# Conditions over another queue, other sums of magnitudes, two-term mixing and unread products in the first tile of an octonion ternary FFN

## Chip, cores and metric

One core of a Trainium2 chip runs the whole kernel. The metric is device time in microseconds of an execution. Three executions of the kernel before took 722.28 to 724.03 us, median 723.83.

## The reference, cut to what matters

```python
xc   = einsum('bct,bcd->bdt', x, weights[condition])      # x: 32 x 64 x 1024, one 64 x 64 matrix per batch entry
Wq   = scale * clip(round(W / scale), -1, 1)              # scale = mean(|W|), for w_gate, w_up, w_down
M    = einsum('jik,jod->koid', S_OCT, Wq)                 # octonion structure constants, 8 x 8 x 8
gate, up = xp @ M_gate, xp @ M_up                         # 1024 -> 2732 each
h    = silu(gate) * up
out  = x + hp @ M_down                                    # 2732 -> 1024
```

Every weight is first replaced by -1, 0 or 1 times the mean magnitude of its whole matrix, so no table of weights can be built before all magnitudes of that matrix are summed.

## The kernel before

The 2048 token rows are 8 tiles of 256. A tile goes through three stages: y (x times the condition's matrix), 12 chunks of gate and up, and the down products. The order of every engine is written out by hand; semaphores join them.

Weights: at the start w_gate (three windows, from ACT's queue) and w_up (three windows) and w_down (one transfer, both from SP's queue) come in as f32. `sum_abs` sums magnitudes (ACT, L672; one window of w_up on DVE, L906), PE adds the partitions (L968), DVE makes the scales (`scales`), then ternary f16 weights (`ternary`, L747 and L749) and from these tables of sums of two weights (`build_table`, L723 to L768). The tables of windows 1 and 2 are made between the first tile's chunks. w_down's ternary weights are combined on PE (`mix`, L981): each mix is four results, each a sum of four ternary blocks with signs, written as products with the identity or its negative; ACT copies them to `down_u` (L667), and scales 16 blocks to `down_c` (L705, `CORR_AFTER`).

y: `y_round(T, r)` (L1003) is 8 f32 products; ACT copies and squares them (`copy_y`, L588, L591), PE sums the squares (`row_norms`, L1010), DVE makes the tile's scales. POOL forms sums of y (`sum_y`, L531), ACT the high f16 parts (`y_hi`, L601), DVE the low parts (`y_lo`, L816). The four conditions of a tile are 64 x 64 blocks loaded into `cond_bd` by an index read from memory (`load_one_cond`, L457, L458); in tile 0 two come from SP's queue and two from ACT's.

Chunk c: PE makes shared products (`shared_pair`, `shared`) and own products (`own`, gate group then up group of 16, all L1016). DVE adds them (p, L723; gate and up, L843), ACT applies silu (L652), DVE multiplies (L870), and one chunk later ACT and DVE split the result into a high and low f16 part (L613, L825). POOL and DVE form sums z of these over groups of chunks; `z_hi` (ACT, L632) and `z_lo` (DVE, L830). The down products are L1108. In the first tile only, `first_tile_at(c, half)` puts y rounds of tile 1 and the 12 mixes before (half 0) or after (half 1) the own products of a chunk.

Of the kernel before, what the change touches and what calls it, by code (L numbers as in the profile page):

```python
# [159 lines left out]
def build(nc, x, cond, cond_w, w_gate, w_up, w_down, out, count):  # L160
# [16 lines left out]

    Y_AT_FIRST = {(1, 1): 0, (2, 1): 1, (3, 0): 2, (3, 1): 3}
    NORM_AT_FIRST = (4, 1)
# [8 lines left out]
    Z_LO_AFTER_FIRST = {8: 0, 9: 1, 10: 2, 11: 3}  # L188
    CORR_AFTER = (8, 9, 10, 11)
    MIX_AT = [(c, half) for c in range(6, 12) for half in range(2)]  # L190
# [24 lines left out]
    with ExitStack() as ctx:  # L215
# [44 lines left out]
        raw_down_at = z_op_f16[:, 2 * NQ * raw_n:].bitcast(F32)  # L260
        raw_down = [of_window(raw_down_at, w) for w in range(NQ)]
        tern_down_at = o_sb[:].rearrange("p a t -> p (a t)")[:, 0:NQ * raw_n // 2].bitcast(F16)
        tern_down = tern_down_at.rearrange("p (w j o) -> p w j o", w=NQ, j=8)
# [77 lines left out]
        idx_loaded = sem("idx_loaded")  # L341
        cond_loaded = sem("cond_loaded")
        x_loaded = sem("x_loaded")
        residual_loaded = [sem(f"residual_loaded_{s}") for s in range(SUB)]
# [11 lines left out]
        tern_ready = [sem("gate_tern_ready"), sem("up_tern_ready"), sem("down_tern_ready")]  # L356
        slots_built = [sem("gate_slots_built"), sem("up_slots_built")]
        down_mixed = sem("down_mixed")
        down_c_ready = sem("down_c_ready")
# [61 lines left out]
        for (h, v), f in F_SIGN.items():  # L421
            for r in range(4):
                r1, r0 = divmod(r, 2)
                terms = []
                for a in range(2):
                    first = 4 * (h ^ v) + 2 * a
                    sign = f[2 * a] * (1, parity(r1))[a]
                    other = parity(r0) if f[2 * a] == f[2 * a + 1] else -parity(r0)
                    terms += [(first, sign), (first + 1, sign * other)]
                mixes[h, v, r] = sorted(terms, key=lambda t: -t[1])  # L430
        MIXES = [(w, h, v) for w in range(NQ) for h, v in F_SIGN]
# [22 lines left out]

        def load_one_cond(eng, T, b):
            h = b % 2
            which = eng.value_load(idx_sb[0:1, T * BPT + b:T * BPT + b + 1], min_val=0, max_val=cond_w.shape[0] - 1)  # L457
            eng.dma_start(cond_bd[C * h:C * h + C, b // 2, C * h:C * h + C],  # L458
                          cond_w[bass.ds(which, 1), :, :].rearrange("a c d -> (a c) d")).then_inc(cond_loaded, 16)

# [3 lines left out]
        def _(sp):  # L464
# [6 lines left out]
            def load_cond(T):  # L471
                for b in range(BPT):
                    load_one_cond(sp, T, b)

# [13 lines left out]
            load_x(0)  # L488
            sp.wait_ge(idx_loaded, 16)
            sp.wait_ge(cond_zeroed, 1)  # L490
            for b in range(BPT // 2):
                load_one_cond(sp, 0, b)
            for w in range(NQ):
                sp.dma_start(raw[1][w], w_up[:, w]).then_inc(up_loaded[w], 16)
            sp.dma_start(raw_down_at, w_down.rearrange("p w j o -> p (w j o)")).then_inc(down_loaded, 16)
            load_x(1)
            load_cond(1)
            sp.wait_ge(down_mixed, len(MIXES))
# [20 lines left out]
        def _(pool):  # L519
# [6 lines left out]
            for dst, value in ((ident, 1.0), (minus_ident, -1.0)):  # L526
                pool.affine_select(out=dst[:], in_=dst[:], compare_op=ALU.not_equal, fill=value, base=0,
                                   pattern=[[-1, P]], channel_multiplier=1).then_inc(ident_set, 1)

            def signed_add(dst, a, b, sign):  # L530
# [52 lines left out]
        def _(act):  # L583
# [36 lines left out]
            def z_hi(T, k):  # L620
                if k == NR - 1:
                    act.wait_ge(z_ready_dve, T + 1)
                else:
                    act.wait_ge(z_ready, (NR - 1) * T + k + 1)
                if T == 0 and k % 2 == 0:


                    for m in range(2):
                        act.wait_ge(slots_built[m], NBUILD * min(NQ, k + 2))
                    if k > 0:  # L630
                        act.wait_ge(tern_ready[2], NQ)
                act.activation(z_op[:, k, 0], z_of(k), ACT.Copy).then_inc(z_hi_ready, 1)  # L632
# [40 lines left out]

            def sum_abs_of(m, w):
                act.wait_ge((gate_loaded, up_loaded)[m][w], 16)
                sum_abs(NQ * m + w, raw[m][w].rearrange("p j o -> p (j o)"), raw_n, abs_sum[m][:, w:w + 1])

            for w in range(NQ):
                act.dma_start(raw[0][w], w_gate[:, w]).then_inc(gate_loaded[w], 16)
            act.wait_ge(idx_loaded, 16)  # L680
            act.wait_ge(cond_zeroed, 1)
            for b in range(BPT // 2, BPT):
                load_one_cond(act, 0, b)
            act.wait_ge(ones_set, 1)
            act.activation(warm, ones[:, 0:1], ACT.Silu)
            for w in range(NQ):
                sum_abs_of(0, w)
            for r in range(4):
                copy_y(0, r)
            for w in range(NQ - 1):  # L690
                sum_abs_of(1, w)
            y_hi(0)
            act.wait_ge(down_loaded, 16)
            sum_abs(2 * NQ - 1, raw_down_at, NQ * raw_n, abs_sum[2])

            corr_list = list(corr.items())
            per_chunk = -(-len(corr_list) // len(CORR_AFTER))
            for T in range(NT):
                for c in range(NC):
                    chunk(T, c)  # L700
                    if T == 0 and c in CORR_AFTER:
                        act.wait_ge(tern_ready[2], NQ)
                        i = per_chunk * CORR_AFTER.index(c)
                        for (h, v, p), (_, ((j, eight),)) in corr_list[i:i + per_chunk]:
                            act.activation(down_c[:, :, v, p, h, :], tern_down[:, :, j, :], ACT.Copy,  # L705
                                           scale=float(eight)).then_inc(down_c_ready, 1)
# [14 lines left out]
        def _(dve):  # L721
# [176 lines left out]
            def ternary_of(m, w):  # L898
                ternary(m, w, tern[m][w], raw[m][w], next(n_tern))

            scales(0)
            ternary_of(0, 0)
            build_table(0, 0)
            y_scales(0)
            dve.wait_ge(up_loaded[NQ - 1], 16)
            dve.tensor_reduce(abs_sum[1][:, NQ - 1:NQ], raw[1][NQ - 1].rearrange("p j o -> p (j o)"), AX.X, ALU.add,  # L906
                              apply_absolute_value=True).then_inc(abs_summed_dve, 1)
            scales(1)
            scales_of_ffn()
            h_scales(0)  # L910
            y_lo(0, range(2))
            ternary_of(1, 0)
            build_table(1, 0)
            y_lo(0, range(2, NY))
            ternary_of(0, 1)
            for T in range(NT):
                for c in range(NC):
# [5 lines left out]
                    if T == 0:  # L923
                        if c in TERN_AFTER:
                            ternary_of(*TERN_AFTER[c])
                        if c in TABLE_AFTER:
                            build_table(*TABLE_AFTER[c])
                        if c in DOWN_AFTER:
                            w = DOWN_AFTER[c]
                            ternary(2, w, tern_down[:, w], raw_down[w], next(n_tern))  # L930
                    if T == 0 and c == SCALES_AFTER_FIRST:
                        scales_of_tile(1)
# [30 lines left out]
        def _(pe):  # L963
            def sum_abs(m):
                pe.wait_ge(abs_summed, (NQ, 2 * NQ - 1, 2 * NQ)[m])
                if m == 1:
                    pe.wait_ge(abs_summed_dve, 1)
                pe.matmul(totals(m), ones[:], abs_sum[m], start=True, stop=True).then_inc(totals_ready, 1)  # L968

            def mix(i):  # L970
                w, h, v = MIXES[i]
                pe.wait_ge(tern_ready[2], w + 1)
                if i == 0:
# [5 lines left out]
                for r in range(4):  # L979
                    for t, (j, sign) in enumerate(mixes[h, v, r]):  # L980
                        mm = pe.matmul(bank_mix[:, r, :], (ident if sign > 0 else minus_ident)[:], tern_down[:, w, j, :],  # L981
                                       start=(r == 0 and t == 0), stop=(t == 3), skip_group_check=True)
                mm.then_inc(down_mixed, 1)

            def y_round(T, r):
                if r == 0:
                    pe.wait_ge(x_loaded, 16 * (T + 1))
                    pe.wait_ge(cond_loaded, 16 * BPT * (T + 1))
                if T > 0:
# [152 lines left out]
            def down(T):  # L1142
# [19 lines left out]
                for s in range(SUB):  # L1162
                    down_part(s, down_u_of(2), False, True).then_inc(down_u_done, 1)

            pe.wait_ge(ones_set, 4)
            for r in range(2):
                y_round(0, r)
# [4 lines left out]

            sum_abs(1)
            for T in range(NT):
                for c in range(NC):
# [50 lines left out]
```

## Time and profile before

| | |
|---|---|
| runs, median (lowest to highest) | 723.83 us (722.28 to 724.03) |
| profiled execution | 724.41 us, span 722.6 us |
| PE busy | 687.3 us, 95% |
| DVE, ACT, POOL busy | 538.6, 332.3, 352.5 us |
| chain that ended last | PE 85%, DVE 7%, ACT 3% |
| granted PE clock, mean | 0.987 |

The span runs from the first to the last instruction of the program. A share of busy time is an average over stages. PE's granted clock is given as a part of 2.4 GHz: 0.50 is 1.2 GHz. The timeline of a stretch lists the instructions of each engine in order of time, neighbours of one kind merged, and in brackets how long the engine was idle before the first and what ended that.

### The profile page before, as it was taken

How to read it: one execution, taken by the hardware profiler on the slowest of the kernel's cores; microseconds unless marked ns; L12 is line 12 of the kernel's file. 1: busy time of each engine (PE TensorE's matmuls, PEld its weight loads, DVE VectorE, ACT ScalarE, POOL GpSimd, SP SyncE). 2: the span in 40 equal slices, each digit the busy share in tenths (PEclk: the TensorE clock that was granted, in tenths of full speed). 3: DMA queues.
4: the chain of work that ended last, by engine and by line, in shares of the span. 5: the costliest groups of instructions: out<-in, count | busy, mean ns of one | idle time of the engine just before them, and what ended most of it. 6: DMA issues, size and time to landing. Idle time of an engine off the chain costs nothing.

```text
span 722.6 us, 17130 instructions
## 1 busy us (share of the span) xinstructions
PE 687.3 (95%) x7046; PEld 625.0 (86%) x7046; DVE 538.6 (75%) x867; ACT 332.3 (46%) x530; POOL 352.5 (49%) x409
## 2 busy tenths in 40 slices
PE   3679998999999999999999999999999999999995
PEld 3468887999999989999899999999899998988895
DVE  1898956767876688676877678766877678777877
ACT  5543485155444546255452555344452554434531
POOL 0200557435736466344856356364753357464553
PEclk9799999999999999999999999999999999999999
DMA  8100003021002110031001110031000300021001
GB/s 327 59 2 1 1 2 122 30 89 64 1 2 88 33 61 2 2 118 63 1 2 52 66 63 2 2 117 62 4 1 11 108 2 1 2 88 31 1 2 59
DMA packets 10576, 31.51 MB, mean 44 GB/s; under 512 B 3330, under 2 KB 3330, under 8 KB 10370
## 3 DMA queue, kind: packets, MB, share of 16 engines
q1 hardware_dynamic: 9906, 28.81, 11.2%
q10 hardware_dynamic: 592, 1.61, 0.7%
q8 instruction: 56, 0.92, 0.5%
q14 instruction: 22, 0.18, 0.1%
HBM read 22.02 MB, written 8.39 MB: 42 GB/s over the span
## 4 chain that ended last, share of the span: by engine, by line
PE 85%; DVE 7%; ACT 3%; issue 2%; POOL 1%; DMA 1%; ACTq 0%; DVEq 0%; POOLq 0%
PE ps L1016 58%; PE ps L1108 21%; PE ps L1003 4%; DMA cond_bd<-in_L_cond_weights_dram 1%; DVE pu_sb L723 1%; ACT down_c L705 1%; POOL z_f L531 1%; PE ps L1010 1%; DVE o_sb L443 1%; ACT z_op L632 1%; DVE ps L843 1%; POOL h_pairs L531 1%; DVE z_op L830 0%; ACT ps L652 0%; DVE gate_table L723 0%
## 5 line engine op out<-in xcount | busy, mean ns | idle before, releaser
L1016 PE MATMUL ps<-y_op,gate_table 128*128 128x256 f16 x2112 | 273.0, 275 | 5.7 <-DVE y_op L816 4.2
L1016 PE MATMUL ps<-y_op,up_table 128*128 128x256 f16 x2112 | 270.7, 273 | 0.2 <-DVE up_table L768 0.2
L1016 PEld LDWEIGHTS ps<-y_op,gate_table 128*128 128x128 f16 x2112 | 207.6, 99 | 30.6 <-DVE y_op L816 4.3
L1016 PEld LDWEIGHTS ps<-y_op,up_table 128*128 128x128 f16 x2112 | 207.1, 98 | 25.1 <-DVE up_table L768 0.7
L531 POOL TENSOR_TENSOR h_pairs<-h_f 128x256 f32<-128x256 f32 (+1 forms) x128 | 121.1, 975 | 151.8 <-ACT h_f L618 94.1
L531 POOL TENSOR_TENSOR z_f<-h_pairs 128x512 f32<-128x512 f32 x80 | 102.7, 1305 | 102.6 <-DVE z_op L830 100.8
L652 ACT ACTIVATE ps<-ps,small 128x512 f32<-128x512 f32 x96 | 63.6, 662 | 175.5 <-DVE ps L843 125.4
L443 POOL TENSOR_TENSOR o_sb<-o_sb,wd_sb 128x256 f32<-128x256 f32 (+1 forms) x150 | 88.3, 626 | 92.7 <-DVE wd_sb L891 91.5
L1108 PE MATMUL ps<-down_c,h_op 128*128 128x128 f16 x1536 | 93.1, 220 | 3.0 <-ACT down_c L705 3.0
L723 DVE TENSOR_TENSOR pu_sb<-ps,q_sb 128x512 f32<-128x512 f32 x96 | 65.8, 686 | 38.7 <-ACT q_sb L646 26.0
L1108 PEld LDWEIGHTS ps<-down_c,h_op 128*128 128x128 f16 x1536 | 89.8, 98 | 4.0 <-ACT down_c L705 3.1
L1108 PE MATMUL ps<-down_u,z_op 128*128 128x256 f16 x768 | 90.8, 274 | 1.5 <-DVE z_op L830 1.5
L830 DVE TENSOR_TENSOR z_op<-z_f,z_op 128x1024 f16<-128x1024 f32 x40 | 49.8, 1246 | 44.7 <-ACT z_op L632 44.7
L825 DVE TENSOR_TENSOR h_op<-ps,h_op 128x512 f16<-128x512 f32 x96 | 65.8, 685 | 23.0 <-ACT h_f L618 23.0
L1108 PEld LDWEIGHTS ps<-down_u,z_op 128*128 128x128 f16 x768 | 73.9, 98 | 9.8 <-DVE z_op L830 1.6
L870 DVE SCALAR_TENSOR_TENSOR ps<-pu_sb,small,ps 128x512 f32<-128x512 f32 x96 | 72.4, 755 | 11.5 <-ACT ps L652 1.6
L613 ACT ACTIVATE h_op<-ps 128x512 f16<-128x512 f32 x96 | 57.5, 599 | 35.3 <-DVE ps L870 33.7
L843 DVE TENSOR_TENSOR pu_sb<-ps,pu_sb 128x512 f32<-128x512 f32 x72 | 49.4, 686 | 31.2 <-PE ps L1016 31.0
L632 ACT ACTIVATE z_op<-z_f 128x1024 f16<-128x1024 f32 x40 | 42.1, 1053 | 36.9 <-POOL z_f L531 36.9
L618 ACT ACTIVATE h_f<-ps 128x512 f32<-128x512 f32 x96 | 57.7, 601 | 0.0
L843 DVE TENSOR_TENSOR ps<-ps,pu_sb 128x512 f32<-128x512 f32 x72 | 49.8, 691 | 4.2 <-PE ps L1016 3.2
L1003 PE MATMUL ps<-cond_bd,x_in 128*128 128x128 f32 x256 | 35.3, 285 | 13.3 <-DMA cond_bd<-in_L_cond_weights_dram 11.1
(75 smaller groups left out, 480.7 us busy)
## 6 DMA issues: line engine op xcount, KB each, us to landing
x_in<-in_x_dram SPq DMA_DIRECT2D x8, 1024.0 KB, 5.3
o_sb<-in_x_dram SPq DMA_DIRECT2D x16, 512.0 KB, 3.6
out_dram<-o_sb SPq DMA_DIRECT2D x15, 512.0 KB, 2.7
h_op<-in_L_ffn_w_gate_dram ACTq DMA_DIRECT2D x3, 512.0 KB, 6.8
h_op<-in_L_ffn_w_up_dram SPq DMA_DIRECT2D x3, 512.0 KB, 7.4
z_op<-in_L_ffn_w_down_dram SPq DMA_DIRECT2D x1, 1536.0 KB, 11.4
out_dram<-o_sb SPq DMA_DIRECT2D x2, 256.0 KB, 2.1
cond_bd<-in_L_cond_weights_dram SPq DMA_DIRECT2D x30, 16.0 KB, 3.0
```

The lines of the kernel that those rows point to most:

```text
L443: last = eng.tensor_tensor(dst, dst, wd_sb[:, s, k1, r0, h, :], ALU.add if sign > 0 else ALU.subtract)
L531: return pool.tensor_tensor(dst, a, b, ALU.add if sign > 0 else ALU.subtract)
L613: act.activation(h_op[:, c, :, 0, :], bank_r(s, 0), ACT.Copy).then_inc(h_hi_ready, 1)
L618: act.activation(h_f[:, c], bank_r(s, 0), ACT.Copy).then_inc(h_copied, 1)
L652: act.activation(bank_r(s, 0), bank_r(s, 0), ACT.Silu, scale=gate_scale(T)).then_inc(silu_ready, 1)
L723: return dve.tensor_tensor(dst, a, b, ALU.add if sign > 0 else ALU.subtract)
L825: dve.tensor_tensor(h_op[:, c, :, 1, :], bank_r(s, 0), h_op[:, c, :, 0, :], ALU.subtract).then_inc(h_lo_ready, 1)
L843: return dve.tensor_tensor(dst, bank, pm.broadcast_to([P, 2, TOK]), ALU.add)
L870: dve.scalar_tensor_tensor(out=bank_r(s, 0), in0=u_sb[:], scalar=up_scale(T), in1=bank_r(s, 0), op0=ALU.mult, op1=ALU.mult).then_inc(h_rea ...
L1003: mm = pe.matmul(bank_y(T, r)[:, i, P * s:P * s + P], x_in[:, s, f:f + P], cond_bd[:, s, :], start=True, stop=True)
L1016: mm = pe.matmul(dst, table[m][:, slot, q, :], y_op[:, op, e, :], start=(i == 0 and e == 0), stop=(i == len(terms) - 1 and e == 1))
L1108: mm = pe.matmul(banks[bank][:, place], operand[:, P * s:P * s + P], weights, start=(bank not in begun), stop=(last and i == ends[bank]), ...
```

## The change

It does six things. (1) The four conditions of tile 0 are issued by POOL, after its set-up, with a semaphore of their own; SP and ACT issue none, and SP goes straight on to w_up and w_down. (2) DVE sums the magnitudes of w_up's windows 0 and 1 before all else, ACT that of window 2 after the copies of y. (3) DVE's order up to the first chunk is changed. (4) Rounds of y for tile 1 stand at other places, all before the own products. (5) DVE adds and subtracts neighbouring ternary blocks of w_down (`down_pairs`), and a mix is a sum of two terms in place of four; the waits of `z_hi` follow from where `down_pairs` lies. (6) Corrections are 6, 5 and 5 behind chunks 8, 9 and 10, in place of 4 behind each of 8 to 11; and PE makes 14 products of 512 columns before y and 4 behind the sum for w_up, into a bank whose content nobody reads.

```diff
-    Y_AT_FIRST = {(1, 1): 0, (2, 1): 1, (3, 0): 2, (3, 1): 3}
+    Y_AT_FIRST = {(1, 0): 0, (2, 0): 1, (3, 0): 2, (4, 0): 3}
-    CORR_AFTER = (8, 9, 10, 11)
+    CORR_AFTER = {8: range(0, 6), 9: range(6, 11), 10: range(11, 16)}
...
+        down_pairs = [raw_down_at[:, w * raw_n:w * raw_n + raw_n // 2].bitcast(F16).rearrange("p (j o) -> p j o", j=8)
+                      for w in range(NQ)]
...
-                    first = 4 * (h ^ v) + 2 * a
+                    pair = 2 * (h ^ v) + a
-                    terms += [(first, sign), (first + 1, sign * other)]
-                mixes[h, v, r] = sorted(terms, key=lambda t: -t[1])
+                    terms.append((pair if other > 0 else 4 + pair, sign))
+                mixes[h, v, r] = terms
...
             load_x(0)
-            sp.wait_ge(idx_loaded, 16)
-            sp.wait_ge(cond_zeroed, 1)
-            for b in range(BPT // 2):
-                load_one_cond(sp, 0, b)
             for w in range(NQ):
                 sp.dma_start(raw[1][w], w_up[:, w]).then_inc(up_loaded[w], 16)
...
+            pool.wait_ge(idx_loaded, 16)
+            pool.wait_ge(cond_zeroed, 1)
+            for b in range(BPT):
+                load_one_cond(pool, 0, b, first_cond_loaded)
...
-                if T == 0 and k % 2 == 0:
+                if T == 0 and k < NQ:
                     for m in range(2):
-                        act.wait_ge(slots_built[m], NBUILD * min(NQ, k + 2))
-                    if k > 0:
-                        act.wait_ge(tern_ready[2], NQ)
+                        act.wait_ge(slots_built[m], NBUILD * (k + 1))
+                elif T == 0:
+                    act.wait_ge(down_mixed, 4 * (k - NQ + 1))
...
-            act.wait_ge(idx_loaded, 16)
-            act.wait_ge(cond_zeroed, 1)
-            for b in range(BPT // 2, BPT):
-                load_one_cond(act, 0, b)
...
             for r in range(4):
                 copy_y(0, r)
-            for w in range(NQ - 1):
-                sum_abs_of(1, w)
+            sum_abs_of(NQ, 1, NQ - 1)
             y_hi(0)
...
+            for w in range(NQ - 1):
+                dve.wait_ge(up_loaded[w], 16)
+                dve.tensor_reduce(abs_sum[1][:, w:w + 1], raw[1][w].rearrange("p j o -> p (j o)"), AX.X, ALU.add,
+                                  apply_absolute_value=True).then_inc(abs_summed_dve, 1)
             scales(0)
             ternary_of(0, 0)
             build_table(0, 0)
             y_scales(0)
-            dve.wait_ge(up_loaded[NQ - 1], 16)
-            dve.tensor_reduce(abs_sum[1][:, NQ - 1:NQ], raw[1][NQ - 1].rearrange("p j o -> p (j o)"), AX.X, ALU.add,
-                              apply_absolute_value=True).then_inc(abs_summed_dve, 1)
             scales(1)
+            ternary_of(1, 0)
+            y_lo(0, range(2))
+            build_table(1, 0)
+            y_lo(0, range(2, NY))
             scales_of_ffn()
             h_scales(0)
-            y_lo(0, range(2))
-            ternary_of(1, 0)
-            build_table(1, 0)
-            y_lo(0, range(2, NY))
             ternary_of(0, 1)
...
                             ternary(2, w, tern_down[:, w], raw_down[w], next(n_tern))
+                            dve.wait_ge(tern_ready[2], w + 1)
+                            t = tern_down[:, w]
+                            for place, sign in ((slice(0, 4), 1), (slice(4, 8), -1)):
+                                signed_add(down_pairs[w][:, place], t[:, 0::2], t[:, 1::2], sign).then_inc(down_paired, 1)
...
-                        mm = pe.matmul(bank_mix[:, r, :], (ident if sign > 0 else minus_ident)[:], tern_down[:, w, j, :],
-                                       start=(r == 0 and t == 0), stop=(t == 3), skip_group_check=True)
+                        mm = pe.matmul(bank_mix[:, r, :], (ident if sign > 0 else minus_ident)[:], down_pairs[w][:, j, :],
+                                       start=(r == 0 and t == 0), stop=(t == 1), skip_group_check=True)
...
+            def unread(n):
+                for _ in range(n):
+                    pe.matmul(ps[:, 5, 0:4 * P], ones_bf[:], ones_bf[:].rearrange("p (a o) -> p a o", a=1)
+                              .broadcast_to([P, 4, P]), start=True, stop=True)
+
             pe.wait_ge(ones_set, 4)
+            unread(14)
             for r in range(2):
                 y_round(0, r)
             sum_abs(0)
...
             sum_abs(1)
+            unread(4)
```

## Rows read from the trace of the kernel before

**Rows 1.** The waits of PE, 136 to 722 us: releaser, us in total, times, longest.
```profile
PE ps L1108 <- DVE z_op L830: 1.5, 1, 1.5
```

**Rows 2.** The waits of PE, 0 to 140 us.
```profile
PE ps L1003 <- ACT y_sq L591: 2.2, 1, 2.2
```

**Rows 3.** The timeline, 75 to 120 us: start, us, instruction, idle before.
```profile
84.97 2.17 DVE L749 SCALAR_TENSOR_TENSOR o_sb<-z_op,small,o_sb 128x1024 f16<-128x1024 f32 x1
...
87.07 0.68 DVE L723 TENSOR_TENSOR pu_sb<-ps,q_sb 128x512 f32<-128x512 f32 x1
...
90.12 1.75 ACT L705 ACTIVATE down_c<-o_sb 128x384 f16<-128x384 f16 x4
...
92.84 1.22 DVE L830 TENSOR_TENSOR z_op<-z_f,z_op 128x1024 f16<-128x1024 f32 x1 [2.41 <-ACT z_op L632]
...
93.98 0.68 DVE L723 TENSOR_TENSOR pu_sb<-ps,q_sb 128x512 f32<-128x512 f32 x1
...
112.56 2.95 PE L1108 MATMUL ps<-down_c,h_op 128*128 128x128 f16 x32 [2.98 <-ACT down_c L705]
```

**Rows 4.** The timeline, 0 to 36 us, and chunk 3's gate products.
```profile
2.95 1.84 SPq L458 DMA_DIRECT2D cond_bd<-in_L_cond_weights_dram  x2
...
4.83 1.53 SPq L494 DMA_DIRECT2D h_op<-in_L_ffn_w_up_dram  x3
...
11.06 3.58 PE L1003 MATMUL ps<-cond_bd,x_in 128*128 128x128 f32 x16 [11.06 <-DMA cond_bd<-in_L_cond_weights_dram]
...
14.80 0.16 DVE L729 TENSOR_REDUCE small<-ps 128x1 f32<-128x3 f32 x1 [14.80 <-PE ps L968]
...
19.29 4.12 POOL L531 TENSOR_TENSOR y_f<-y_f 128x256 f32<-128x256 f32 x5 [16.88 <-DVE gate_table L768]
...
20.13 1.21 DVE L906 TENSOR_REDUCE small<-h_op 128x1 f32<-128x1024 f32 x1
...
23.72 2.47 DVE L816 SCALAR_TENSOR_TENSOR y_op<-y_f,small,y_op 128x1024 f16<-128x1024 f32 x2
...
26.25 3.60 PE L1016 MATMUL ps<-y_op,gate_table 128*128 128x256 f16 x16 [4.20 <-DVE y_op L816]
26.89 1.28 DVE L749 SCALAR_TENSOR_TENSOR z_op<-h_op,small,z_op 128x1024 f16<-128x1024 f32 x1
...
28.21 1.16 DVE L723 TENSOR_TENSOR up_table<-z_op 128x512 f16<-128x512 f16 x4
...
29.92 1.80 DVE L816 SCALAR_TENSOR_TENSOR y_op<-y_f,small,y_op 128x1536 f16<-128x1536 f32 x1
...
34.47 0.69 DVE L723 TENSOR_TENSOR pu_sb<-ps,q_sb 128x512 f32<-128x512 f32 x1 [0.76 <-PE ps L1016]
...
51.64 3.39 PE L1016 MATMUL ps<-y_op,gate_table 128*128 128x256 f16 x16
```

**Rows 5.** The waits of DVE, 0 to 66 us.
```profile
DVE small L729 <- PE ps L968: 15.5, 2, 14.8
DVE pu_sb L843 <- PE ps L1016: 2.0, 2, 1.2
DVE ps L843 <- PE ps L1016: 1.9, 1, 1.9
```

**Rows 6.** Issue to landing, us: x's (last number), then w_up's, then the conditions'.
```profile
x_in<-in_x_dram SPq DMA_DIRECT2D x1, 1024.0 KB, 8.1
...
DMA to landing us min/median/max: 6.7/7.4/8.2
...
DMA to landing us min/median/max: 2.0/5.0/7.0
```

**Rows 7.** Stretches: PE, PEld, DVE, ACT, POOL busy, granted clock, DMA share, GB/s.
```profile
50.00:60.00 10.00, 9.35 (x70) 7.93 (x71) 6.83 (x16) 5.42 (x12) 0.00 (x0) 0.83 0.01 2
...
113.00:136.00 23.00, 23.00 (x290) 21.53 (x288) 16.68 (x17) 8.04 (x10) 9.56 (x9) 0.93 0.28 96
```

**Rows 8.** The chain of waits, 80 to 90 us: start, us, what.
```profile
81.39 0.89 PE ps L981 x16
```

More of the change, by code:

```diff
@@ L342, in build @@
         cond_loaded = sem("cond_loaded")
+        first_cond_loaded = sem("first_cond_loaded")
         x_loaded = sem("x_loaded")
@@ L357, in build @@
         slots_built = [sem("gate_slots_built"), sem("up_slots_built")]
+        down_paired = sem("down_paired")
         down_mixed = sem("down_mixed")
@@ L458, in load_one_cond @@
             eng.dma_start(cond_bd[C * h:C * h + C, b // 2, C * h:C * h + C],
-                          cond_w[bass.ds(which, 1), :, :].rearrange("a c d -> (a c) d")).then_inc(cond_loaded, 16)
+                          cond_w[bass.ds(which, 1), :, :].rearrange("a c d -> (a c) d")).then_inc(loaded, 16)
         block = ctx.enter_context(nc.Block())
@@ L472, in load_cond @@
                 for b in range(BPT):
-                    load_one_cond(sp, T, b)
+                    load_one_cond(sp, T, b, cond_loaded)
             def rows(T, s):
@@ L496, in _ @@
             load_x(1)
+            sp.wait_ge(idx_loaded, 16)
+            sp.wait_ge(cond_zeroed, 1)
             load_cond(1)
@@ L672, in sum_abs, with sum_abs_of @@
                 act.activation(junk[:, 0:size], src, ACT.Abs, accum_out=dst).then_inc(abs_summed, 1)
-            def sum_abs_of(m, w):
+            def sum_abs_of(n, m, w):
                 act.wait_ge((gate_loaded, up_loaded)[m][w], 16)
-                sum_abs(NQ * m + w, raw[m][w].rearrange("p j o -> p (j o)"), raw_n, abs_sum[m][:, w:w + 1])
+                sum_abs(n, raw[m][w].rearrange("p j o -> p (j o)"), raw_n, abs_sum[m][:, w:w + 1])
             for w in range(NQ):
                 act.dma_start(raw[0][w], w_gate[:, w]).then_inc(gate_loaded[w], 16)
-            act.wait_ge(idx_loaded, 16)
-            act.wait_ge(cond_zeroed, 1)
-            for b in range(BPT // 2, BPT):
-                load_one_cond(act, 0, b)
             act.wait_ge(ones_set, 1)
@@ L686, in _ @@
             for w in range(NQ):
-                sum_abs_of(0, w)
+                sum_abs_of(w, 0, w)
             for r in range(4):
                 copy_y(0, r)
-            for w in range(NQ - 1):
-                sum_abs_of(1, w)
+            sum_abs_of(NQ, 1, NQ - 1)
             y_hi(0)
             act.wait_ge(down_loaded, 16)
-            sum_abs(2 * NQ - 1, raw_down_at, NQ * raw_n, abs_sum[2])
+            sum_abs(NQ + 1, raw_down_at, NQ * raw_n, abs_sum[2])
             corr_list = list(corr.items())
-            per_chunk = -(-len(corr_list) // len(CORR_AFTER))
             for T in range(NT):
@@ L702, in _ @@
                         act.wait_ge(tern_ready[2], NQ)
-                        i = per_chunk * CORR_AFTER.index(c)
-                        for (h, v, p), (_, ((j, eight),)) in corr_list[i:i + per_chunk]:
+                        for i in CORR_AFTER[c]:
+                            (h, v, p), (_, ((j, eight),)) = corr_list[i]
                             act.activation(down_c[:, :, v, p, h, :], tern_down[:, :, j, :], ACT.Copy,
@@ L964, in sum_abs @@
             def sum_abs(m):
[L965 removed]
+                pe.wait_ge(abs_summed, NQ + m)
                 if m == 1:
[L967 removed]
+                    pe.wait_ge(abs_summed_dve, NQ - 1)
                 pe.matmul(totals(m), ones[:], abs_sum[m], start=True, stop=True).then_inc(totals_ready, 1)
@@ L971, in mix @@
                 w, h, v = MIXES[i]
-                pe.wait_ge(tern_ready[2], w + 1)
+                pe.wait_ge(down_paired, 2 * (w + 1))
                 if i == 0:
@@ L987, in y_round @@
                     pe.wait_ge(x_loaded, 16 * (T + 1))
-                    pe.wait_ge(cond_loaded, 16 * BPT * (T + 1))
+                    if T == 0:
+                        pe.wait_ge(first_cond_loaded, 16 * BPT)
+                    else:
+                        pe.wait_ge(cond_loaded, 16 * BPT * T)
                 if T > 0:
```

2 lines of the change are left out of this document (1 added, 1 removed).

## The prediction

> **What bounds the kernel now.** I read the waits of TensorE (PE) first, in two stretches. After the first tile PE waits once, 1.5 us in total [rows 1]; every other wait of weight lies in the first 136 us, as 2.2 us for a square of y [rows 2]; the timelines give the rest in brackets: 3.0 us for down_c [rows 3], 11.1 for the first conditions, 4.2 for y's operands [rows 4]. From the first down product at 112.56 us [rows 3] on, PE has no gap, so the end moves by what that product moves, plus changes of PE's clock around it. The diff touches nothing behind it. The question is thus: how much earlier does down(0) start?
>
> Ahead of it, the timeline by engine shows who carries the chain. VectorE (DVE) starts at 14.80 us [rows 4] and then waits for PE's sum only once, 15.5 - 14.8 = 0.7 us, before the scales of up. Then PE and DVE alternate; in chunks 3 and 4 DVE waits for PE 1.9 us, and twice more, 2.0 together [rows 5]. In chunks 5 to 7 DVE never waits. In chunks 8 to 11 it waits for ScalarE (ACT) before every z_lo, 2.41 us in the first [rows 3]: silu, mix copy, four corrections, z_hi, then z_lo, then the next chunk. That loop takes 93.98 - 87.07 = 6.9 us.
>
> **Start of the chain.** x, ahead of all else on SP's queue, lands 8.1 us after its issue [rows 6], so past 9. The four conditions go out from 2.95 on, two on each queue, and take up to 7.0 us; PE starts at 11.06 [rows 4, 6]. The first 16 y products take 3.58 us, and PE granted at full level would take half: I read it as its lower level, 1.2 GHz. DVE's first scale stands behind them: 11.06 to 14.80 = 3.74 us. In the new kernel two sums of 1.21 us stand ahead of it on DVE. The second of the three up transfers is issued near 5.3 (three in the 1.53 us from 4.83) and takes 7.4 us, landing at 12.7 [rows 4, 6]; the queues are already full of earlier bytes, so the earlier issue in the new order shifts the landing little. 12.7 + 1.21 = 13.9; I take 14.0 against 14.80: 0.8 us gained. This holds if the conditions land by 14.0 - 3.74 = 10.3. No row shows a transfer issued by GpSimd (POOL). Bounds: four issues in a row at SP's pace (4.83 - 2.95 over two = 0.94 each) from 2.4, when POOL's last set-up ends, give 6.2; with the fastest landing of a condition, 2.0, they are there at 8.2, and x decides, past 9; with the slowest, 7.0, at 13.2, 2.9 too late. I take the median landing of 5.0: 11.2, and then count on the 14 unread products: they start at about 1.7 us, 0.43 us each at 1.2 GHz, and if they bring PE to 2.4 GHz the first 16 take 1.8 instead of 3.6, so that 12.1 is early enough. So 0 cost, bounds 0 and +2.9.
>
> The Trainium skill ("DMA: Bandwidth & Descriptors", SWDGE vs HWDGE vs iDMA) says that a POOL transfer has its descriptors written in software and that plain transfers belong on SP or ACT; its latency section gives about 1 us against 0.6 to the first byte. By that figure the conditions would be some 0.4 us later, inside the slack above. No run here shows it yet.
>
> **To y and chunk 0.** Out of DVE's chain go the sum of up's third window (1.21 us [rows 4], now on ACT at about 17, behind the copies of y) and the hole of 0.7, since the totals are now there early. The ffn and h scales (about ten small instructions, the scales of up among them, stand between the hole's end at 22.1 and 23.72; 1.1 us is theirs) move behind the last y_lo. The ternary of up (2.1 us) moves ahead of the first two y_lo. y_lo 0 starts at 23.72 - 0.8 - 1.2 - 0.7 - 1.1 + 2.1 = 22.0. POOL's sums of y (4.12 us) follow the gate table and now lie beside that ternary. The same ternary step took 1.28 us alone and 2.17 us beside POOL in chunk 7 [rows 3, 4]; bounds 0 and 0.9, I take 0.5. Two y_lo: 2.47. Ready at 25.0; PE's first gate group started at 26.25. The table of up (28.21 to 29.92: 1.8 with its wait) is ready at 26.8, the last y_lo (1.8) at 28.6 (before 31.7) [rows 4]. Scales and ternary(0,1) leave DVE free at 31.8.
>
> PE decides chunk 0. sum_abs(1) and its four unread products are over by 20, then PE idles until 25. In the trace it idled 4.2 us there and the first 16 products took 3.60 us, the lower level. I take the same fall. Then gate ends at 28.6, PE rises near 30, up ends at 31.1, the 16 shared ones at 32.85. DVE's chunk 0 starts at 32.85 against 34.47: **-1.6 us** (bounds: -2.7 if PE stays at 2.4 GHz and DVE decides, 0 if the rise comes 1.7 later).
>
> The Trainium skill ("SBUF — State Buffer", Who interferes with whom) says that a DVE instruction with two SBUF inputs and a POOL one that reads SBUF exclude each other. The 1.28 and 2.17 us agree. By it the ternary could wait for a whole POOL instruction, about 0.8 us, instead of my 0.5.
>
> **Chunks 0 to 5.** The first pairing adds two 128x512 f16 additions; four such take 1.16 [rows 4], two with their wait 0.6, on DVE with nothing beside: **+0.6 us** (bounds 0.5 and 0.8). y's first round of tile 1 now stands ahead of own(1) and waits for the scales of down, 3.2 us after chunk 0 begins: PE idles some 2.2 us there. Queued behind it is own(1), whose gate result DVE wants only 9 us after chunk 0 begins (chunk, scales, table, ternary, pairing), so it is late for nobody even at 1.2 GHz. In return rounds 1, 2 and 3 stand ahead of own(2), own(3), own(4), each a chunk half after ACT's squares: PE no longer holds for the square (2.2 us idle [rows 2], after which 16 products took 3.39 us [rows 4], with a mean granted clock of 0.83 from 50 to 60 [rows 7], that is 3.4 us at 0.50). By my walk own(3)'s gate is ready 2 us before DVE asks. So the waits 1.9 + 2.0 [rows 5] go, with rounding **-3.85 us**; the bound on the other side is 0, if the clock falls elsewhere or the hole only moves. I take the upper end, since 2 us of slack stand at each of three chunks. What is late next is DVE itself.
>
> **Chunks 6 and 7.** Two more pairings on DVE's chain, 0.6 each, now beside POOL, which has begun on z; 0.3 more each for the exclusion: **+1.8 us** (bounds +1.1 and +2.6).
>
> **Chunks 8 to 11.** Half of the mixing products go: 16 took 0.89 us [rows 8], so 12 x 0.44 = 5.3 us of PE. All of it is hidden: ACT's loop is the longer. Bounds 0 and -0.8. Corrections 4,4,4,4 become 6,5,5,0. One is 1.75/4 = 0.44 us [rows 3]: chunks 8, 9, 10 lengthen by 0.88 + 0.44 + 0.44 = 1.75, and the last four, which down(0) awaited, go with their 1.75. Net **0**. Next late is the copy of the last mix, 1.7 us earlier in its chunk. z_hi's new waits are on mixes long done; POOL's sums for tile 1 had some 5 us of slack before PE's second tile and keep over 3.
>
> **Sum.** -1.6 + 0.6 - 3.85 + 1.8 + 0 = -3.05 us. Against the profiled execution's 724.41 (span 722.6 and 1.8 around it) that is 721.4; the median of the runs is 0.6 lower, so **720.8**.
>
> **Rivals.**
> (B) The hole of chunks 3 and 4 does not go but moves: an idle PE at y's first round (2.2 us, as long as the one that half speed followed) brings the fall there. Then -1.6 + 0.6 + 1.8 = +0.8: 724.6, or anything between. For it: same length of idling. Against: slack of 2 us.
> (C) PE keeps 2.4 GHz where it lost it: at 25 (another -1.1, DVE decides) and behind 112.56, where the mean clock of 0.93 over 23 us [rows 7] is 3.2 us at 0.50, a loss of 1.6. -3.05 - 1.1 - 1.6 = -5.75: 718.1. For it: the unread products and shorter waits. Against: PE idles 5 us before y, and 2.3 us before down.
> (A) **Slower: POOL's issues decide.** Place: the four conditions. Each us after 10.3 (12.1 with PE at full speed) goes straight through y, first scale and DVE's chain. The gain of 3.05 is gone when they land at 13.4 (15.2); at 16 the time is 723.83 + 16 - 10.3 - 3.05 = 726.5. It needs about 3 us per issue from 2.4 on. For it: the four stand in a row on one queue and no row prices one. Against: nothing else is on POOL's queue then, and DVE is idle until 12.
>
> **Chances.** Forecast 0.45 (own range 719.6 to 722.3), B 0.20, C 0.25, A 0.10. About 0.3% (2.2 us) is what a measurement of this kernel can tell from no change; faster means below 721.7. Forecast gives 0.37 faster and 0.08 same, C 0.25 faster, B 0.20 same, A half same and half slower: 0.62, 0.33, 0.05. Range 717.8 (C) to 724.1 (most of B).
>
> **What would show it.** Conditions landed by 10.3 to 12.1; DVE's first scale at 14.0 and no hole before the second; first gate product at 25.0; chunk 0 on DVE at 32.9; no DVE wait for PE in chunks 3 and 4; the chunk loops 8 to 10 of 7.8, 7.3 and 7.3 us; down(0) at 109.5, released by the last mix copy. Wrong it would be made by a first y product behind 13, a clock at 0.50 between 35 and 60, or pairings of over a us.

## The result: slower by half a per cent

The changed kernel took 726.79 us (median, 725.95 to 727.35) against 722.88 us for the kernel before (722.08 to 724.03), each executed six times. The ratio is 1.0051, 95% interval 1.0039 to 1.0063: 3.7 us slower, where 3.05 us faster was forecast. Its profiled execution took 726.86 us, span 725.1. The waits of PE from 0 to 140 us in the profile after (columns as in [rows 2]):

```profile
PE ps L988 <- ACT down_u L675: 8.9, 6, 2.7
PE ps L1026 <- DVE y_op L818: 6.6, 1, 6.6
PE ps L1013 <- DMA cond_bd<-in_L_cond_weights_dram: 5.0, 1, 5.0
PE ps L1013 <- DVE small L735: 2.4, 1, 2.4
PE ps L1118 <- ACT down_u L675: 2.2, 1, 2.2
```

The wait for a square of y [rows 2] is gone and so is down_c's. In their place PE waits 8.9 us for copies of mixes: in chunks 6 to 11 PE is the engine that waits, not the one that sets the pace. After 136 us it waits 1.5 us once, as before [rows 1], so the loss lies in the first tile here too. The timeline of the changed kernel's start, answering to [rows 4]:

```profile
1.82 5.40 PE L1179 MATMUL ps<-ones_bf 128*128 128x512 bf16 x14 [1.82 <-POOL minus_ident L527]
...
3.69 0.66 POOL L463 DMA_DIRECT2D cond_bd<-in_L_cond_weights_dram  x1 [1.16 <-issue]
...
4.87 0.52 POOL L463 DMA_DIRECT2D cond_bd<-in_L_cond_weights_dram  x1 [0.51 <-issue]
...
6.01 0.52 POOL L463 DMA_DIRECT2D cond_bd<-in_L_cond_weights_dram  x1 [0.62 <-issue]
...
7.15 0.52 POOL L463 DMA_DIRECT2D cond_bd<-in_L_cond_weights_dram  x1 [0.63 <-issue]
...
12.23 3.75 PE L1013 MATMUL ps<-cond_bd,x_in 128*128 128x128 f32 x16 [5.01 <-DMA cond_bd<-in_L_cond_weights_dram]
12.61 1.22 DVE L905 TENSOR_REDUCE small<-h_op 128x1 f32<-128x1024 f32 x1 [0.16 <-DMA h_op<-in_L_ffn_w_up_dram]
...
16.24 0.16 DVE L731 TENSOR_REDUCE small<-ps 128x1 f32<-128x3 f32 x1 [2.42 <-PE ps L975]
...
20.73 5.42 POOL L539 TENSOR_TENSOR y_f<-y_f 128x256 f32<-128x256 f32 x5 [13.07 <-DVE gate_table L770]
20.86 1.02 PE L1179 MATMUL ps<-ones_bf 128*128 128x512 bf16 x4
...
22.20 1.71 DVE L749 TENSOR_SCALAR z_op<-h_op,small 128x1024 f16<-128x1024 f32 x1
23.95 1.62 DVE L751 SCALAR_TENSOR_TENSOR z_op<-h_op,small,z_op 128x1024 f16<-128x1024 f32 x1
25.50 2.93 DVE L818 SCALAR_TENSOR_TENSOR y_op<-y_f,small,y_op 128x1024 f16<-128x1024 f32 x2
...
28.49 3.60 PE L1026 MATMUL ps<-y_op,gate_table 128*128 128x256 f16 x16 [6.60 <-DVE y_op L818]
...
36.51 0.69 DVE L725 TENSOR_TENSOR pu_sb<-ps,q_sb 128x512 f32<-128x512 f32 x1 [1.54 <-PE ps L1026]
```

Read it in order. POOL's four issues start 1.14 us apart and the first only at 3.69; the last one's condition lets y begin at 12.23, not at 11.06. The 14 unread products end at 7.2, PE then idles 5.01 us, and the 16 y products take 3.75 us, the lower level (1.2 GHz) as before. So the first scale is at 16.24, with a hole of 2.42 us ahead of it on DVE, where 14.0 was forecast. Then three DVE steps fall under POOL's sums of y (20.73 on): 1.71, 1.62 and 2.93 us, where the kernel before had 0.75, 1.28 and 2.47.

DVE in chunks 6 to 9 of the changed kernel, answering to [rows 3]:

```profile
79.12 0.74 DVE L749 TENSOR_SCALAR o_sb<-z_op,small 128x1024 f16<-128x1024 f32 x1
79.89 1.63 DVE L751 SCALAR_TENSOR_TENSOR o_sb<-z_op,small,o_sb 128x1024 f16<-128x1024 f32 x1
81.55 1.70 DVE L725 TENSOR_TENSOR z_op<-o_sb 128x512 f16<-128x512 f16 x2
83.17 0.68 DVE L725 TENSOR_TENSOR pu_sb<-ps,q_sb 128x512 f32<-128x512 f32 x1
...
86.77 1.59 DVE L749 TENSOR_SCALAR o_sb<-z_op,small 128x1024 f16<-128x1024 f32 x1
88.39 2.17 DVE L751 SCALAR_TENSOR_TENSOR o_sb<-z_op,small,o_sb 128x1024 f16<-128x1024 f32 x1
90.60 0.76 DVE L725 TENSOR_TENSOR z_op<-o_sb 128x512 f16<-128x512 f16 x2
91.27 0.68 DVE L725 TENSOR_TENSOR pu_sb<-ps,q_sb 128x512 f32<-128x512 f32 x1
...
97.81 1.23 DVE L832 TENSOR_TENSOR z_op<-z_f,z_op 128x1024 f16<-128x1024 f32 x1 [3.17 <-ACT z_op L640]
```

A pairing is two additions, 0.76 us where POOL does not run beside it, 1.70 where it does; and the ternary step beside it (0.75 before, in chunk 7) now takes 1.59. The start of each of DVE's chunks, read from rows like these, and that of the first down product (down(0), on PE) give the ledger (us; "base" is the kernel of the experiments `y_places_and_corrections` and `base_again`, the latter's profile):

| chunk | 0 | 1 | 2 | 3 | 4 | 5 | 6 | 7 | 8 | 9 | 10 | 11 | down(0) |
|---|---|---|---|---|---|---|---|---|---|---|---|---|---|
| before | 34.47 | 41.66 | 47.01 | 52.00 | 60.45 | 68.25 | 73.60 | 80.91 | 87.07 | 93.98 | 100.91 | 107.77 | 112.56 |
| changed | 36.51 | 44.49 | 49.84 | 55.43 | 60.97 | 68.77 | 74.12 | 83.17 | 91.27 | 98.95 | 106.29 | 113.56 | 116.76 |
| changed - before | 2.0 | 2.8 | 2.8 | 3.4 | 0.5 | 0.5 | 0.5 | 2.3 | 4.2 | 5.0 | 5.4 | 5.8 | 4.2 |
| base | 34.19 | 41.38 | 46.74 | 51.72 | 56.99 | 64.80 | 70.15 | 77.47 | 83.62 | 91.37 | 98.71 | 105.98 | 109.18 |

Chunk 0 starts 2.0 us late, the three pairings add 0.8, 1.7 and 1.9, the y rounds give back 2.9 in chunk 3, and the corrections cost 1.6 and return it. That makes 3.5; the other 0.6 arise in chunk 2, where the kernel before has no wait:

```profile
39.81 1.45 PE L1013 MATMUL ps<-cond_bd,x_in 128*128 128x128 f32 x8 [2.40 <-DVE small L735]
41.05 3.29 PE L1026 MATMUL ps<-y_op,gate_table 128*128 128x256 f16 x16
...
52.26 0.69 DVE L845 TENSOR_TENSOR pu_sb<-ps,pu_sb 128x512 f32<-128x512 f32 x1 [0.53 <-PE ps L1026]
```

PE idles 2.40 us ahead of y's first round, then falls to its lower level (mean granted clock 0.57 from 40 to 44 us; the 16 gate products of chunk 1 take 3.29 us, and 1.91 at the higher level), and DVE still waits for it in chunk 2. This is rival B of the prediction, in part.

In this pair of profiles 1.7 of the 4.2 us come back behind 116.76: the first 32 down products took 1.95 us where they took 2.95 [rows 3], and the next 32 start 3.53 us behind them and not 5.19, PE being at its higher level.

### The profile page after: what moved, and what is told of

Same layout as the page of the kernel before. It is cut to its first block, busy times and chain, and to the rows that moved or that the text cites. A ratio compares the mean times of both kernels' runs of the same rounds, so it can differ in the third digit from the quotient of the medians.

```text
span 725.1 us, 16979 instructions
## 1 busy us (share of the span) xinstructions
PE 688.7 (95%) x6968; PEld 621.4 (86%) x6968; DVE 546.4 (75%) x874; ACT 331.7 (46%) x528; POOL 355.2 (49%) x413
## 4 chain that ended last, share of the span: by engine, by line
PE 85%; DVE 6%; ACT 3%; issue 2%; POOL 1%; DMA 1%; POOLq 0%; DVEq 0%; ACTq 0%
PE ps L1026 59%; PE ps L1118 21%; PE ps L1013 4%; ACT down_c L707 1%; PE ps L1020 1%; DVE pu_sb L725 1%; POOL z_f L539 1%; DVE o_sb L448 1%; ACT z_op L640 1%; DMA cond_bd<-in_L_cond_weights_dram 1%; DVE ps L845 1%; DVE ps L872 1%; DVE o_sb L751 1%; POOL h_pairs L539 1%; DVE z_op L832 0%
## 5 line engine op out<-in xcount | busy, mean ns | idle before, releaser
L539 POOL TENSOR_TENSOR y_f<-y_f 128x256 f32<-128x256 f32 (+1 forms) x40 | 41.0, 1048 | 13.7 <-DVE gate_table L770 13.1
```

The costliest lines, as they stand in the source:

```text
L539: return pool.tensor_tensor(dst, a, b, ALU.add if sign > 0 else ALU.subtract)
```

## The experiments

"Share of before" is the ratio of times to the kernel before on the same chip, with its 95% interval; 0.1% is 0.72 us. The first four undo one part of the changed kernel (its own share: 1.0051).

**Conditions back on SP's and ACT's queues.**

```diff
-            for b in range(BPT): load_one_cond(pool, 0, b, first_cond_loaded)
+            for b in range(BPT // 2): load_one_cond(sp, 0, b, first_cond_loaded)      # behind load_x(0)
+            for b in range(BPT // 2, BPT): load_one_cond(act, 0, b, first_cond_loaded) # behind w_gate
```

> The changed kernel with part 1 undone: two conditions from SP's queue and two from ACT's, as before. Theory (the start waits for POOL's conditions): y's first product comes back from 12.2 to about 11.1 us and DVE's first scale from 16.2 to 14.8 to 15.1, so the kernel is 1.0 to 1.4 us faster than the changed one: 725.4 to 725.8. Rival (the conditions hide behind up's two sums on DVE, which end at 13.8, and something later decides): under 0.3 us, 726.5 to 726.8.

Measured 1.0019 (1.0005 to 1.0032), 725.21 us: 2.3 us better than the changed kernel. y starts at 10.82, the first scale at 14.83, chunk 0 at 34.21, 2.3 us earlier. The rival (the conditions hide behind up's two sums) is out. The price is more than the 1.4 us at the first scale; part of it is made between the scale and chunk 0, where chunk 0 waited for PE 1.5 us in the changed kernel and 0.6 here, the gate products being 3.60 and 3.52.

**Mixes of four terms, no pairing.**

```diff
-                            for place, sign in ((slice(0, 4), 1), (slice(4, 8), -1)):
-                                signed_add(down_pairs[w][:, place], t[:, 0::2], t[:, 1::2], sign).then_inc(down_paired, 1)
...
-                        mm = pe.matmul(..., down_pairs[w][:, j, :], ...)   # 2 terms
+                        mm = pe.matmul(..., tern_down[:, w, j, :], ...)    # 4 terms
```

> The changed kernel with part 5 undone: no pairing on DVE, mixes of four terms on PE. Theory (DVE carries the chain in chunks 0, 6 and 7, and each pairing costs 0.8 to 1.7 us there, with what it pushes under POOL): DVE's chunk 8 starts 3.5 to 4.2 us earlier, down(0) too, and the time is 722.6 to 723.3. Rival (PE needs the 5.3 us of shorter mixes in chunks 6 to 11, so the pairing pays for itself): 726 or more.

Measured 0.9985 (0.9976 to 0.9994), 722.66 us: 4.8 us better, by itself enough to make the rest slightly faster than before. Chunk 8 starts at 86.79 in place of 91.27. The halved mixes bought nothing that the whole ones lack. Not all of the 4.8 us is the pairings', though. In this profile chunk 0 starts at 35.71, 0.8 us earlier before any pairing is made, and chunk 4 follows it after 24.45 us, with the first pairing after 24.46: PE fell behind y's first round in both, and what the missing pairing leaves free DVE spends in waiting for PE. The other 3.7 us lie in chunks 6 and 7.

**Sums and DVE's order as before.**

```diff
-            for w in range(NQ - 1): dve.wait_ge(up_loaded[w], 16); dve.tensor_reduce(abs_sum[1][:, w:w + 1], ...)
...
-            scales(1); ternary_of(1, 0); y_lo(0, range(2)); build_table(1, 0); y_lo(0, range(2, NY)); scales_of_ffn(); h_scales(0)
+            dve.tensor_reduce(abs_sum[1][:, NQ - 1:NQ], ...)
+            scales(1); scales_of_ffn(); h_scales(0); y_lo(0, range(2)); ternary_of(1, 0); build_table(1, 0); y_lo(0, range(2, NY))
```

> The changed kernel with parts 2 and 3 undone: magnitudes and DVE's order up to the first chunk as before, conditions still from POOL. Theory (the new order gains the sum and the hole, but its ternary and its first y_lo fall under POOL's sums of y: 1.71, 1.62 and 2.93 us for 0.74, 1.28 and 2.47): the two nearly cancel, first gate product within 0.7 us of the changed kernel's 28.5, time 726.0 to 727.3. Rival A (the order is worth the 2.5 us that its instructions say): 1.5 to 2.5 us slower than the changed kernel, over 728. Rival B (the order is itself the loss): 725.5 or less.

Measured 1.0034 (1.0022 to 1.0046), 726.06 us: 1.2 us better, with intervals that touch. The first gate product is at 27.39 in place of 28.49; 0.3 of these 1.1 us lie ahead of the first scale already (15.93 and 16.24). The order is not worth the 2.5 us that its instructions say (rival A is out), and is nearer to a loss.

**Without the unread products.**

```diff
-            unread(14)
...
-            unread(4)
```

> The changed kernel without the 18 unread products. Theory (they bring nothing: the first 16 y products took 3.75 us with them and 3.58 without, the first gate group 3.60 and 3.60): time within 0.5 us of the changed kernel, 726.3 to 727.3. Rival A (they keep PE at 2.4 GHz somewhere, as from 20.6 to 27 us): 1 us or more slower. Rival B (they hold PE's queue at y's start): 0.5 to 1 us faster.

Measured 1.0049 (1.0035 to 1.0063): no difference. The first 16 y products took 3.75 us and the first gate group 3.60, both ways.

The next ones build up from the kernel before.

**The places of y's rounds alone.**

```diff
-    Y_AT_FIRST = {(1, 1): 0, (2, 1): 1, (3, 0): 2, (3, 1): 3}
+    Y_AT_FIRST = {(1, 0): 0, (2, 0): 1, (3, 0): 2, (4, 0): 3}
```

> The kernel before with only part 4: rounds of y for tile 1 ahead of own(1), own(2), own(3), own(4). Theory (this part alone takes away the hole of 2.2 us on PE, the fall of the clock behind it and 3 us of DVE's waits in chunk 3; in all four kernels that have it chunk 3 to 4 takes 5.55 us against 8.45): 2.5 to 4 us faster than before, 720 to 721.5. Rival (the hole only moves to y's first round, where PE waits 2.4 us for the scales of down and falls to 1.2 GHz): within 1 us of before.

Measured 0.9973 (0.9962 to 0.9984), 721.33 us: 2.0 us faster (the median of 721.33 suggests more). In its profile chunk 3 takes 5.28 us in place of 8.45 and down(0) starts at 109.39 in place of 112.56, and the clock stays at 1.00 from 40 to 60 us. The rival's wait stands at y's first round, 2.40 us, but in this profile the 16 gate products behind it take 1.91 us and DVE sees nothing of it. That is not so in every execution, as the two profiles of the next kernel show; of the eleven of this one, seven took 720.8 to 721.5 us at a mean clock of 0.989 to 0.991, four 722.5 to 724.3 at 0.983 to 0.987.

**Places of y and corrections.**

```diff
-    CORR_AFTER = {8: range(0, 4), 9: range(4, 8), 10: range(8, 12), 11: range(12, 16)}
+    CORR_AFTER = {8: range(0, 6), 9: range(6, 11), 10: range(11, 16)}
```

> The kernel before with parts 4 and the corrections of part 6 (6, 5, 5, 0). Theory (what the three longer chunk loops of ACT cost, 1.2 to 1.7 us, the missing four at the end give back): within 0.5 us of the kernel with part 4 alone. Rival (PE's shorter wait before the down products keeps it at 2.4 GHz there, where the kernel before lost 1.6 us): 1 to 1.6 us faster than part 4 alone.

> The kernel with y's places and the corrections only, timed again as the base of the other three. Its runs so far fell into two groups, 719.5 (mean granted clock 0.994) and 721 to 721.8 (0.989). Expected: ratio to before 0.993 to 0.996, about 3 to 4.5 us faster than before. Rival (the gain over y's places alone was luck of three good runs): ratio 0.9965 or more.

Measured 0.9943 (0.9930 to 0.9955) and, a second time, 0.9953 (0.9940 to 0.9965): 3.4 to 4.1 us faster than before, and the fastest kernel found. The start of down(0) is no earlier than with y's places alone; what differs is PE behind it. First its first 32 down products with y's places alone, then with the corrections moved:

```profile
109.39 3.21 PE L1115 MATMUL ps<-down_c,h_op 128*128 128x128 f16 x32 [2.97 <-ACT down_c L709]
```

```profile
109.18 1.95 PE L1115 MATMUL ps<-down_c,h_op 128*128 128x128 f16 x32 [1.72 <-ACT down_u L672]
```

PE waits 1.72 us in place of 2.97 and comes out at its higher level; the next 32 start 3.53 us behind the first and not 4.79. The two stretches 105 to 125 us (columns: length, PE busy, granted clock, DMA share, GB/s), in the same order:

```profile
105.00:125.00 20.00, 17.03 (x217) 0.91 0.31 110
```

```profile
105.00:125.00 20.00, 18.28 (x253) 1.00 0.30 110
```

The fall costs 4.79 - 3.53 = 1.26 us in these rows; the ratios give 1.4 to 2.2. The rival is right: what the corrections bring is the clock behind the wait, not an earlier down(0). All six profiles with a wait of 1.7 us ahead of down(0) have 1.95 us for the first 32 products, the two with 3.0 us have 2.95 and 3.21. In between the length of the wait does not decide alone: behind 2.16 us five profiles have 1.95 and one 2.50.

The two profiles of this one kernel also show what rival B of the prediction is worth. The second (719.32 us) is "base" in the ledger; the first took 721.84 us. Its down(0) comes at 111.67, 2.5 us later, the whole difference. Of that 0.85 stand at chunk 0 (35.04 and 34.19; the first gate group took 3.60 and 3.30 us), and 1.7 in chunks 1 to 3, where its PE fell behind y's first round:

```profile
38.34 1.24 PE L1010 MATMUL ps<-cond_bd,x_in 128*128 128x128 f32 x8 [2.40 <-DVE small L737]
39.38 3.51 PE L1023 MATMUL ps<-y_op,gate_table 128*128 128x256 f16 x16
```

In the second profile the idling is the same 2.40 us, and the 16 products take 1.91 us.

**Sums and DVE's order with early conditions.** The base with parts 2 and 3 added.

```diff
-            dve.tensor_reduce(abs_sum[1][:, NQ - 1:NQ], ...)                 # behind y_scales(0)
+            for w in range(NQ - 1): dve.tensor_reduce(abs_sum[1][:, w:w + 1], ...)   # ahead of scales(0)
```

> Parts 2, 3, 4 and the corrections, with conditions as before, mixes of four terms and no unread products. It tells what the sums and DVE's order are worth once the conditions are early. Theory (the order gains little, since its ternary and first y_lo fall under POOL's sums of y): DVE's chunk 0 within 0.5 us of 34.4 and the time within 0.7 us of the kernel with parts 4 and corrections alone. Rival A (the order was only held up by the late conditions): 1.5 us or more faster than that one. Rival B (it is a loss of 1 us or more by itself).

Measured 0.9962 (0.9949 to 0.9974), 721.20 us. Chunk 0 starts at 34.25 (base 34.19 and 35.04). The first two y_lo take 2.94 us here too. It is 0.6 to 1.4 us behind the base's two measurements, inside the intervals of one and not of the other: no gain, and whether it is a loss stays open.

**POOL held back** while DVE makes the pairings.

```diff
-                    pool.wait_ge(slots_built[1], NQ * NBUILD)
+                    pool.wait_ge(down_paired, 2 * NQ)
```

> The changed kernel with POOL's first z round held until the last pairing is done (it began beside ternary and pairing of w_down's window 1). Theory (DVE's two-input instructions lose to POOL's on what they share): without POOL beside them the ternary steps take 0.74 and 1.28 us again instead of 1.59 and 2.17, each pairing 0.6 to 0.8 us for two instead of 1.70, and DVE's chunk 8 starts 2.3 to 3 us earlier, near 88.5; z is then late and ACT waits for it in chunk 8, so the time is the same or worse. Rival (the instructions are slow for where their operands lie): durations unchanged.

DVE in chunks 6 to 9 of this kernel:

```profile
79.41 0.74 DVE L749 TENSOR_SCALAR o_sb<-z_op,small 128x1024 f16<-128x1024 f32 x1
80.18 1.28 DVE L751 SCALAR_TENSOR_TENSOR o_sb<-z_op,small,o_sb 128x1024 f16<-128x1024 f32 x1
81.50 0.76 DVE L725 TENSOR_TENSOR z_op<-o_sb 128x512 f16<-128x512 f16 x2
...
85.78 0.75 DVE L749 TENSOR_SCALAR o_sb<-z_op,small 128x1024 f16<-128x1024 f32 x1
86.56 1.28 DVE L751 SCALAR_TENSOR_TENSOR o_sb<-z_op,small,o_sb 128x1024 f16<-128x1024 f32 x1
87.88 0.76 DVE L725 TENSOR_TENSOR z_op<-o_sb 128x512 f16<-128x512 f16 x2
88.56 0.68 DVE L725 TENSOR_TENSOR pu_sb<-ps,q_sb 128x512 f32<-128x512 f32 x1
...
95.20 1.37 DVE L832 TENSOR_TENSOR z_op<-z_f,z_op 128x1024 f16<-128x1024 f32 x1 [3.27 <-ACT z_op L640]
```

Every instruction has its duration back: 1.59 becomes 0.75, 2.17 becomes 1.28, the pairings are 0.76 each. Chunk 7 takes 6.4 us in place of 8.1, and chunk 8 starts at 88.56 in place of 91.27. The rival (where the operands lie) is out: operands and instructions are the same, only POOL is away. What is left of the two pairings, 0.5 us in chunk 6 and 0.2 in chunk 7 against the kernel before, is their own work, less what POOL had cost there before. As expected z is late and ACT's loop 8 takes 7.9 us in place of 7.7; one execution took 726.42 us, too near the changed kernel's to tell it apart.

**The three disputed parts, each on the base alone.** The diffs are those above the other way round.

> The base with the pairing and the mixes of two terms. Theory (the price of the pairing is DVE's and POOL's and has nothing to do with late conditions): 3.7 to 4.8 us slower than the base, as undoing it in the changed kernel gained 4.8. Rival (it only hurts because everything else is late too): under 2 us.

Measured 1.0001 (0.9992 to 1.0010), 724.55 us: 3.5 us slower than `base_again` (0.48%), a little under the expected 3.7 to 4.8. Chunk 8 starts at 89.49 in place of 83.62, and chunks 6 and 7 alone are longer by 3.5 us. So the price of the pairings in chunks 6 and 7 does not depend on late conditions; the rest of the shift to 89.49 arises up to chunk 3, where this profile, too, has PE at its lower level behind y's first round (3.26 us for the 16 gate products).

> The base with the four conditions issued by POOL. Theory (POOL's issues 1.14 us apart from 3.7 on bring y's first product to 12.2 to 12.5, and nothing hides that, since here no sum on DVE stands ahead of the first scale): 1.0 to 1.6 us slower than the base. Rival (in the changed kernel 2.3 us came back when it was undone, as the clock too was hurt): over 2 us.

Measured 0.9959 (0.9947 to 0.9971), 720.83 us: the interval overlaps the base's 0.9953. In the profiles, both with a mean clock of 0.994, y begins at 12.52 in place of 10.96 and down(0) at 111.06 in place of 109.18, and the executions at that clock took 720.6 to 721.1 us against 719.3 to 719.8. So 1.2 us on equal clocks, as the theory has it, but not shown by the medians, where the base had three executions of six at a mean clock of 0.989, 1.0 to 2.3 us longer, and this kernel one. In the base's two profiles, one from each group, PE falls behind y's first round in the longer and not in the shorter. That every execution of a group is like its profile is not shown.

> The base with the 18 unread products. Theory (they leave PE's level at y and at the first gate group as it was, since PE idles again behind them): within 0.5 us of the base. Rival (with the sums and order of the kernel before, the four behind sum_abs(1) stand only 3 us ahead of the first gate group, near enough to keep it at 2.4 GHz): first gate group 1.9 us in place of 3.6, and 1 us or more faster than the base.

Measured 0.9946 (0.9933 to 0.9958), 719.71 us: the same as the base within the intervals. The four stand close to the first gate group now, and still:

```profile
22.54 1.02 PE L1176 MATMUL ps<-ones_bf 128*128 128x512 bf16 x4
26.89 3.56 PE L1023 MATMUL ps<-y_op,gate_table 128*128 128x256 f16 x16 [3.33 <-DVE y_op L820]
```

PE waits 3.33 us behind them and works at its lower level again.

## Why the prediction was wrong

It named the right stretch and the right carriers and got the sign wrong. The start of down(0) was forecast 3.05 us earlier and came 4.2 later. Of these 7.3 us, 2.2 are the conditions and 1.4 the rest of the way to chunk 0, 2.1 the pairings, 1.0 y's places, and 0.6 the fall behind y's first round; 1.7 us came back behind down(0) in the profiles. By its own steps:

- **Pairings, +0.6 and +1.8: mis-sized by 2.1 us.** They cost 0.8 in chunk 0 and 1.7 + 1.9 in chunks 6 and 7, 4.5 us in the ledger, the largest cost of the change; undone, 4.8 us by the ratios, not all of it theirs, and 3.5 on the base. The step that failed is "0.3 more each for the exclusion". Beside POOL's additions a DVE instruction takes up to 1.0 us longer: the first pairing beside it took 1.70 for 0.76, and the one-input ternary step, which was given no price, 1.59 for 0.75. Holding POOL back gave both their durations back, so the cause is shown. The section of the Trainium skill that I weighed ("SBUF — State Buffer", Who interferes with whom) names that case as well: beside two-input instructions it lists tensor_scalar among those that can enter a mode with both ports and then contend with POOL. The trace agrees, with 1.59 and 0.75; that this instruction ran in that mode is not shown. I had read from the section only the two-input half.
- **Start of the chain, -0.8 and "0 cost" for the conditions: failed.** The first scale came at 16.24, 1.44 late. Two assumptions broke. The issues started at 3.69, not 2.4, as POOL reads each index and then issues, 1.14 us apart; the landing, 5.2 us behind the issue in the median of the four, was near the 5.0 that I took. And the 14 unread products did not bring y to the higher level, and PE idled 5.0 us between them and y. Undone, this part gives 2.3 us in the changed kernel and 1.2 to 1.9 on the base. The rival "POOL's issues decide" had the mechanism at a smaller size, and its break-even of 13.4 was not reached: alone it would not have turned the sign.
- **To y and chunk 0, -1.6: failed, measured +2.0.** Of the difference of 3.6, 2.2 are the start above (16.24 for 14.0). Most of the rest is POOL's sums of y beside three DVE steps: 0.96 + 0.34 + 0.46 = 1.8 us where 0.5 was taken. The hole of 0.7 us did go. With early conditions chunk 0 came to 34.25, no better than with the old order.
- **y's places, -3.85: right in mechanism, the size too large, and "late for nobody even at 1.2 GHz" failed.** Chunk 3 got shorter by 2.9 us; the wait of 0.8 us in chunk 4 stays. Behind the 2.40 us at y's first round PE fell in the changed kernel (0.57 from 40 to 44 us, the prediction's own sign of being wrong) and DVE waited for it, 0.53 us in chunk 2 and 0.22 in chunk 3. It fell in nine of the thirteen profiles with these places, and in the base's slower profile it cost 1.7 us. Rival B, given 0.20, is thus partly right. As the only change, y's places gave 2.0 us by the ratio, 3.2 by the start of down(0).
- **Chunks 8 to 11, net 0: right for the time of down(0)** (loops of 7.7, 7.3 and 7.3 us against 7.8, 7.3, 7.3 forecast; the release by the last mix copy came true). What it missed is rival C's second half: PE stayed at 2.4 GHz behind the shorter wait, 1.7 us in the changed kernel's profile and 1.4 to 2.2 by the ratios of the base.
- **Halved mixes, 0: right.** PE waits 8.9 us in these chunks for copies of mixes.
- **Unread products:** I took them to bring y's products to the higher level and to do nothing for the first gate group. Only the second is true.

The kernel that beats both is the base: y's places and the corrections, and nothing else of the change, 0.9943 to 0.9953 of the time before.

What stays open: whether sums and order with early conditions cost up to 1.4 us or nothing, since their profile's down(0), at 110.63, lies between the base's two (109.18 and 111.67). What decides whether PE falls behind y's first round, and how long its first gate group takes, was not tried: the idling ahead is the same 2.40 and 4.21 us in both profiles of the base.

## What to carry to other kernels

An instruction that moves beside another engine's must be priced with that engine running: take the duration of every kind of instruction that the trace shows in both surroundings, not only of the kind that you suspect, and when the added work lies on the engine that carries the chain, add what it pushes under the neighbour. Taking work off an engine that waits (here mixes on PE) buys nothing and is not worth one instruction on the engine that it waits for. Moving work out of the gap ahead of a long stretch of products can pay in the clock behind it even where, as here, the stretch starts no earlier (109.18 and 109.39). A hole that is moved to another place has to be priced at that place with PE at its lower level. Work that nobody reads, set some microseconds ahead of the products that it should warm, paid nothing in two kernels.

## What the runs showed of the hardware that was not expected

- POOL's four small transfers: issues 1.14 us apart, against 0.94 on SP's queue [rows 4], landing 4.9 to 5.6 us after issue while the queues carried the weights.
- A DVE ternary step of one f32 input of 1024 elements: 0.75 us alone, 1.59 and 1.71 beside POOL's additions; an addition pair of f16 128x512: 0.76 and 1.70.
- PE after 14 products of 512 columns (1.82 to 7.2 us) and an idle 5.0 us gave its next 16 products at 1.2 GHz (3.75 us). After idling 1.7 us ahead of down(0) it stayed at the higher level, after idling 3.0 us it fell (1.95 and 3.21 us for 32 products).
- The length of the idling alone does not tell which: behind 2.40 us ahead of y's first round one kernel gave its 16 gate products in 1.91 us in one execution and in 3.51 in another, and behind 2.16 us ahead of down(0) five profiles have 1.95 us for 32 products and one 2.50.
- One kernel's executions fall into groups by mean clock: the base 719.3 to 719.8 us at 0.994 and 720.8 to 721.6 at 0.989.
